# Long attention of a two-branch layer stack: scores ahead of the transposes, and the copies of transposed blocks exchanged between VectorE and ACT

## The reference

```python
xn = _layernorm(x, axis=-1)
x = x + _L0_attn_ref(xn, ...) + _L0_ffn_ref(xn, ...)

# first branch: causal attention, 8 heads in 2 groups of 4, head width 128, keys of latent width 32
q = (x @ wq).reshape(Bq, Tq, N_KV, N_REP, HEAD_DIM)
k = jnp.einsum('bkhl,ld->bkhd', x @ wk_down ..., wk_up)
v = jnp.einsum('bkhl,ld->bkhd', x @ wv_down ..., wv_up)
scores = jnp.einsum('bqhrd,bkhd->bhrqk', q, k) * scale
scores = jnp.where(causal, scores, jnp.finfo(scores.dtype).min)
probs = jax.nn.softmax(scores, axis=-1)
y = jnp.einsum('bhrqk,bkhd->bqhrd', probs, v)
return y.reshape(Bq, Tq, N_HEADS * HEAD_DIM) @ wo

# second branch: six layers, each window attention (16 heads, window 32, rotary) and a gated feed-forward
for i in range(DEPTH):
    x = attn_layer(shift_tokens(x), ...) + x
    x = ffn_layer(shift_tokens(x), ...) + x
```

## Time and profile before

| what | value |
|---|---|
| three runs | 1828.48, 1821.57, 1826.56 us; median 1826.56 |
| the profiled execution, its own time | 1832.16 us |
| its span in the profile | 1830.4 us |
| TensorE (PE) busy | 1633.6 us, 89% |
| VectorE (DVE) busy | 1517.1 us, 83% |
| ACT busy | 1312.9 us, 72% |
| GpSimd (POOL) busy | 1311.1 us, 72% |
| mean granted TensorE clock | 0.975 |

### The profile page before, as it was taken

The page is one execution under the profiler, slowest core; times in us unless marked ns, Lnnn a source line. Parts: engine busy times, 40 slices in busy tenths (PEclk is TensorE's granted clock), DMA queues, the critical chain, the costliest instruction groups (busy, mean ns, idle before and its releaser), DMA issues.

```text
span 1830.4 us, 72588 instructions
## 1 busy us (share of the span) xinstructions
PE 1633.6 (89%) x31192; PEld 1112.7 (61%) x31192; DVE 1517.1 (83%) x1941; ACT 1312.9 (72%) x1868; POOL 1311.1 (72%) x1287
## 2 busy tenths in 40 slices
PE   6777776788999999999999999999999999999995
PEld 5555665455656666666566666656666666666654
DVE  4466566689988999889899989989899998999973
ACT  2465564567788778777877887778777877887773
POOL 3100001888998888898789988889988899888871
PEclk7899999999999999999999999999999999999998
DMA  6011010010000100000100001000010000000000
GB/s 189 11 37 43 17 36 1 4 56 7 8 14 7 56 8 7 11 15 30 33 8 12 15 7 56 7 10 15 8 39 25 7 12 15 7 7 8 7 7 27
DMA packets 47997, 40.61 MB, mean 22 GB/s; under 512 B 33217, under 2 KB 41153, under 8 KB 46017
## 3 DMA queue, kind: packets, MB, share of 16 engines
q1 hardware_dynamic: 47680, 35.98, 7.0%
HBM read 20.22 MB, written 1.05 MB: 12 GB/s over the span
## 4 chain that ended last, share of the span: by engine, by line
PE 44%; issue 24%; DVE 17%; ACT 7%; POOL 6%; SPq 1%; DMA 0%; DVEq 0%; POOLq 0%; ACTq 0%
PE banks L1170 18%; PE banks L1444 10%; PE banks L1393 5%; PE banks L1468 5%; PE banks L1429 4%; DVE arena L1033 3%; DVE lnx L1095 3%; DVE small L1062 2%; DVE small L1068 2%; DVE small L1056 2%; DVE small L1080 1%; ACT L821 1%; ACT arena L755 1%; DVE arena L1028 1%; ACT L824 1%
## 5 line engine op out<-in xcount | busy, mean ns | idle before, releaser
L1444 PE MATMUL banks<-M,xs 128*32 128x512 f32 x3072 | 368.2, 597 | 0.6 <-ACT arena L755 0.3
L1028 DVE TENSOR_TENSOR arena<-banks,tabs 128x1024 f32<-128x1024 f32 x192 | 233.7, 1217 | 39.6 <-ACT arena L715 23.9
L514 POOL TENSOR_TENSOR arena<-arena 128x1024 f32<-128x1024 f32 x96 | 229.7, 2392 | 46.0 <-DVE arena L1033 45.7
L755 ACT ACTIVATE arena<-banks 128x1024 f32<-128x1024 f32 x192 | 196.9, 1025 | 71.1 <-PE banks L1444 69.8
L1033 DVE TENSOR_TENSOR arena<-banks,tabs 128x1024 f32<-128x1024 f32 x192 | 233.0, 1213 | 0.0
L519 POOL TENSOR_TENSOR arena<-arena 128x1024 f32<-128x1024 f32 x96 | 228.1, 2376 | 0.0
L509 POOL TENSOR_TENSOR prob<-prob,small 128x1024 f32<-128x1024 f32 x96 | 183.8, 1914 | 31.5 <-DVE small L1070 31.5
L1095 DVE SCALAR_TENSOR_TENSOR lnx<-lns,small 128x128 f32<-128x128 f32 x96 | 174.4, 1816 | 34.5 <-POOL small L562 33.5
L1170 PE MATMUL banks<-qkH,xsH 128*128 128x512 f32 x384 | 172.8, 450 | 32.3 <-DVE arena L1033 26.5
L1468 PE MATMUL banks<-arena 128*32 128x128 f32 x6144 | 192.3, 278 | 4.2 <-ACT arena L821 4.2
L574 POOL TENSOR_TENSOR arena<-arena,small 128x1024 f32<-128x1024 f32 x96 | 182.8, 1904 | 9.8 <-POOL arena L519 0.5
(11 more groups left out here) (127 smaller groups left out, 3727.0 us busy)
## 6 DMA issues: line engine op xcount, KB each, us to landing
arena<-in_wvo_dram SPq DMA_DIRECT2D x6, 1024.0 KB, 5.3
qkraw<-in_wqk_dram SPq DMA_DIRECT2D x6, 1024.0 KB, 5.3
gq<-w1w SPq DMA_DIRECT2D x64, 64.0 KB, 2.0
lns<-Xt SPq DMA_DIRECT2D x96, 32.0 KB
lns<-Xt SPq DMA_DIRECT2D x96, 31.8 KB
xsH<-w1w SPq DMA_DIRECT2D x32, 64.0 KB, 2.0
xsL<-w1w SPq DMA_DIRECT2D x32, 64.0 KB, 2.0
W<-in_w_dram SPq DMA_DIRECT2D x6, 341.0 KB, 3.2
```

Of the source, the lines that this page charges most:

```text
L514: pool.tensor_tensor(kc, kc, ks, ALU.add).then_inc(s["k_add"], 1)
L755: act.activation(vw[:, (2 * k + g) % RV, :], two(V_BANK), ACT.Copy).then_inc(s[f"v_cp{g}"], 1)
L1028: dve.tensor_tensor(heads(c), heads(two(0)), table(k % NT, kind), ALU.mult).then_inc(s[done], 1)
L1444: ins = pe.matmul(bk(V_BANK + z)[WIN * q:WIN * (q + 1), :], xs[:, b, t0:t0 + WIN], M[:, q, :, :].rearrange("p m n -> p (m n)"), start=True ...
```

## The change

ACT and VectorE exchange the copies: VectorE copies A, ACT copies B and C. On TensorE the long row's scores of t + 2 come first in a step. On VectorE the copy of A is followed by the long row's maximum (t + 2) and then by the short row's (t + 1), and the bookkeeping of every fourth step comes ahead of these.

```diff
 # ACT
-            def first_blocks(t):
+            def last_blocks(t):
+                nb = row_long(t) - 3
+                act.wait_ge(s["gB_mm"], t + 1)
+                act.activation(gptL[t // REP % 2][:, h, 4:4 + nb, :], bk(bank_of(("B", t, 0)))[:, 0:P * nb]..., ACT.Copy).then_inc(s["gB_cp"], 1)
+            def short_blocks(t):
+                nb = row_short(t) + 1
+                act.wait_ge(s["gC_mm"], t + 1)
+                act.activation(gptS[t // REP % 2][:, h, 0:nb, :], bk(bank_of(("C", t, 0)))[:, 0:P * nb]..., ACT.Copy).then_inc(s["gC_cp"], 1)
...
                     if t % REP == 2 and t >= REP:
                         inverses(t // REP - 1)
-                    first_blocks(t)
+                    last_blocks(t)
+                    short_blocks(t)
                     if t + 1 < NSTEP:
                         exp_short(t + 1)
 # VectorE
-            def last_blocks(t):
-            def short_blocks(t):
+            def first_blocks(t):
+                dve.wait_ge(s["gA_mm"], t + 1)
+                dve.tensor_copy(gptL[t // REP % 2][:, h, 0:4, :], bk(bank_of(("A", t, 0)))...).then_inc(s["gA_cp"], 1)
...
                 if t % REP == 0 and t:
                     reciprocals(t // REP - 1)
-                if t + 1 < NSTEP:
-                    peak_short(t + 1)
                 if t % REP == 0 and t >= 2 * REP:
                     add_outputs(t // REP - 2)
                 if t % REP == 2 and t >= REP:
                     scale_outputs(t // REP - 1)
+                first_blocks(t)
                 if t + 2 < NSTEP:
                     peak_long(t + 2)
-                last_blocks(t)
-                short_blocks(t)
+                if t + 1 < NSTEP:
+                    peak_short(t + 1)
 # TensorE
             for t in range(NSTEP):
+                if t + 2 < NSTEP:
+                    score_long(t + 2)
                 turn_first(t)
                 turn_last(t)
                 if t + 1 < NSTEP:
                     score_short(t + 1)
-                if t + 2 < NSTEP:
-                    score_long(t + 2)
                 turn_short(t)
```

More of the change, by code:

```diff
@@ L681, in exp_short @@
                                accum_out=gsum[t // REP % 2][:, REP + h:REP + h + 1]).then_inc(s["gS_exp"], 1)
-            def first_blocks(t):
+            def last_blocks(t):
                 it, p, h = long_at(t)
-                act.wait_ge(s["gA_mm"], t + 1)
-                act.activation(gptL[t // REP % 2][:, h, 0:4, :], bk(bank_of(("A", t, 0))).rearrange("p (k t) -> p k t", k=4), ACT.Copy)\
-                   .then_inc(s["gA_cp"], 1)
+                nb = row_long(t) - 3
+                act.wait_ge(s["gB_mm"], t + 1)
+                act.activation(gptL[t // REP % 2][:, h, 4:4 + nb, :], bk(bank_of(("B", t, 0)))[:, 0:P * nb].rearrange("p (k t) -> p k t", k=nb),
+                               ACT.Copy).then_inc(s["gB_cp"], 1)
+            def short_blocks(t):
+                it, p, h = long_at(t)
+                nb = row_short(t) + 1
+                act.wait_ge(s["gC_mm"], t + 1)
+                act.activation(gptS[t // REP % 2][:, h, 0:nb, :], bk(bank_of(("C", t, 0)))[:, 0:P * nb].rearrange("p (k t) -> p k t", k=nb),
+                               ACT.Copy).then_inc(s["gC_cp"], 1)
             def inverses(q):
@@ L943, in peak_short @@
                 dve.tensor_reduce(gmx[:, 2:3], bk(6)[:, 0:n], AXX, ALU.max, negate=True).then_inc(s["gS_max"], 1)
-            def last_blocks(t):
+            def first_blocks(t):
                 it, p, h = long_at(t)
[L947 to L950, removed]
-            def short_blocks(t):
[L953 to L957, removed]
+                dve.wait_ge(s["gA_mm"], t + 1)
+                dve.tensor_copy(gptL[t // REP % 2][:, h, 0:4, :], bk(bank_of(("A", t, 0))).rearrange("p (k t) -> p k t", k=4))\
+                   .then_inc(s["gA_cp"], 1)
             def reciprocals(q):
```

## The result

The changed kernel took 1771.34 us (median of 4 runs, 1768.50 to 1772.87) against 1827.52 for the kernel before beside it: 0.9694 of its time, 95% interval 0.9665 to 0.9723. The profiled execution took 1768.50 us, with a span of 1766.7.

What follows compares the result with a forecast made beforehand. Bound: TensorE waiting for VectorE's copy of the long row's last blocks. Savings of 34.9 us in 14 stretches plus 3 in the first five steps make 38, giving 1788.5 us after a 5.6 median correction; range 1776 to 1812.

Steps and rivals of the forecast that it cites:

- What bounds the kernel: Long attention: TensorE's transposes wait 40.2 us for VectorE's copy of the last blocks; a microsecond saved there shortens the total.
- The walk's stretches: Long attention, four steps from weighing to weighing without a unit: 12.2 us instead of 14.69, 34.9 saved over 14.
- the ring given for p = 0: Row pair 0: a two-step loop of waits through TensorE, VectorE and ACT takes 4.94 us, steps 2.5 in the mean.
- The first five steps: Start of the long attention, at a mixed clock: 0.6 us saved each, 3 in all (0 to 5).
- a unit costs 2.1: Key and query units in eleven places of the 14 stretches: 2.1 us each, left unchanged.
- The single costs: Instruction lengths: ACT's one-block copy 0.28 us, VectorE's four-block copy 0.68, ACT's work per step some 2.15.
- The bookkeeping: VectorE's add, scale and reciprocals every fourth step, moved ahead: costed at nothing, 0.4 in four steps if not covered.
- (a): ACT's instructions don't overlap in successive copies: 0.2 us a step, 10 to 12 over the stage, 1799; chance 0.15.
- (b): Key or query units wait for ACT's copy: 1.15 us for each of 12, 14 less saved, 1802.5; chance 0.14.
- (c): TensorE becomes the bound in the long attention, its own work 10.5 us per four steps, 1765; chance 0.10.
- (d): TensorE at its lower clock: four steps 16.7 us, +28 over 14 stretches, 1854; chance 0.07.
- (e): The long attention's gain doesn't reach the end: order on TensorE unchanged or later layers eat it, 1826.5; chance 0.04.

Runs made afterwards that it cites:

- e0: The kernel before, unchanged, run again for a second profile; ratio 1.000 (0.9986 to 1.0015).
- e11: The changed kernel, unchanged, run again on another occasion against the kernel before; 1773.58 us, ratio 0.9684.
- e7: The change in steps 0 to 5 alone, the kernel before's arrangement from step 6 on, against the kernel before; 1815.83 us, ratio 0.9920.
- e9: The kernel before, but VectorE copies the long row's remaining blocks ahead of the long maximum, no copy changes engine; 1801.18 us, ratio 0.9843.
- e6: The kernel before with four unused products of 512 columns added on TensorE in each of steps 0 to 4; 1829.27 us, ratio 0.9997.
- e2: The changed kernel's copies and VectorE and ACT order, with TensorE's order of before, against the kernel before; 1791.95 us, ratio 0.9787.
- e3: The changed kernel, but TensorE keeps long scores behind short ones in steps 0 to 5, against the kernel before; 1776.22 us, ratio 0.9700.

## Why the prediction was wrong

The profiled executions of e0 (span 1829.4) and e11 (1774.0) differ by 55.4 us, close to the difference of the medians. Their parts:

| part | forecast | measured | from |
|---|---|---|---|
| steps 0 to 5, to the first weighing | 3 | 11.4 | 65.50 - 54.08; first profiles 15.3; e7 14.4 |
| 14 stretches, without what units cost | 34.9 | 32.5 | 204.8 - 172.3: four each of 14.44 and 14.02, three each of 15.11 and 15.20; now of 12.05, 12.48, 12.82, 11.90 |
| eleven units in them | 0 | 6.2 | 22.2 - 16.0: six in pairs at 4.17 a pair, three at 1.90, two at 2.02; now 3.14, 1.08, 1.68 |
| drops of the clock before | 0 | 4.7 | e0's stretches over those of the earlier trace rows |
| the rest | 0 | 0.6 | 55.4 less the above |

- **What bounds the kernel** held: the copy of B behind the long maximum was the wait (e9 frees it and gains 29 us), and what is saved arrives at the end.
- **The walk's stretches** held: 12.2 in the mean against 12.31. That 11.9 for p = 0 meets 11.90 and 12.5 for p = 3 meets 12.48 is luck in part: the walk took four steps of one p, and a stretch from weighing to weighing has two steps of one p and two of the next (0 and 1, then 2 and 3). And the ring given for p = 0 was the wrong one. Ordinary steps there take 2.20, not 2.5. This did no harm, since behind a weighing the walk itself had steps of 2.18; TensorE is the bound there, busy 11.04 of 11.90 us.
- **The step that failed first**: "The first five steps run at a mixed clock; 0.6 each, 3 in all (0 to 5)". 0.6 is the gain of a stretch divided by four. But in a stretch one step of four had nothing to gain, because the weighing already covered its wait: before, A follows the weighing without idle time (120.61), and after, L comes in between and moves it 0.57 later. The first weighing stands at the end of step 5, so the steps ahead of it gain what an ordinary one does, up to 3.91 - 2.20 = 1.7 at p = 0, and five units lie among them. The clock adds a part: it is 0.82 and 0.69 in the two profiles of before, 0.95 and 0.94 in those of after. The rows had that in them: the prediction read a clock of 0.9 or more in nearly all of the long attention, while the first two of its seven slices, 0 to 91 us, show 7 and 8. How the 11 to 15 us divide is not settled: e6's trace gives the clock 4 to 7 and leaves 7.5 to 9.2 to the arrangement; e6's time gives it at most 3.5.
- **The second**: a unit costs 2.1, "and I leave that as it is". It costs (15.19 - 12.05) / 2 = 1.6 now, 1.1 at step 13 of sixteen (13.56 - 12.48; before 15.92 - 14.02 = 1.9), 1.7 at step 4 (13.58 - 11.90; before 17.22 - 15.20 = 2.0). The stretches of before with the unit of step 13 and with that of step 4:

```profile
87.05:102.97 15.92, 12.03 (x151) 9.79 (x150) 11.03 (x22) 9.95 (x23) 0.00 (x0) 1.00 0.26 63
118.08:135.30 17.22, 11.59 (x152) 9.73 (x151) 10.63 (x21) 9.61 (x23) 0.00 (x0) 1.00 0.01 2
```

Before, the product of the unit behind step 22 waited 1.60 us for B's bank, whose copy stood behind the long maximum; now it follows C at once, and L and A fill the time in which ACT and VectorE finish the unit. The timelines of this unit before, then after:

```profile
141.30 1.12 PE L1170 MATMUL banks<-arena 128*128 128x512 f32 x2 [1.60 <-DVE arena L949]
142.26 0.60 PE L1311 MATMUL banks<-cst,prob 128*128 128x128 f32 x4
143.84 0.55 PE L1311 MATMUL banks<-cst,prob 128*128 128x128 f32 x3 [0.98 <-DVE xnw L904]
```

```profile
113.08 1.02 PE L1170 MATMUL banks<-arena 128*128 128x512 f32 x2
113.54 0.92 PE L1170 MATMUL banks<-xnw,xsL 128*128 128x512 f32 x2
...
114.35 0.62 PE L1311 MATMUL banks<-cst,prob 128*128 128x128 f32 x4
115.76 0.55 PE L1311 MATMUL banks<-cst,prob 128*128 128x128 f32 x3 [0.79 <-DVE xnw L913]
```

- **The third**, small: the stretches of before at a clock below 1.00 were left out of the sum. They cost 4.7 us in e0 and 2.4 in the first profile (16.66 and 18.07 against 15.11 and 17.22). After, every stretch from the first weighing on is at 1.00.
- **The single costs** held: ACT copies one block in 0.27 to 0.29 (L694 and L687; 0.28 taken), VectorE copies four in 0.69. The bookkeeping was rightly put at nothing. ACT is busy 133.03 of 180 us between 70 and 250, 74%, not above 80%: 2.15 us in a step of 2.5 are 86%, but ACT also stands in every weighing, and four times 2.15 in a stretch of 12.2 are 71%.
- **The rivals.** (a) ACT's instructions don't overlap: they do. In ACT's timeline of after each row starts 0.10 or 0.11 before the one ahead of it ends; C's copy, for one, starts 0.48 into B's copy of 0.59:

```profile
203.76 0.37 ACT L680 ACTIVATE arena<-banks,small 128x128 f32<-128x128 f32 x1 [0.60 <-DVE small L952]
204.03 0.19 ACT L680 ACTIVATION_READ_ACCUMULATOR arena<-banks,small 128x1 f32 x1
204.12 1.10 ACT L672 ACTIVATE prob<-banks,small 128x1024 f32<-128x1024 f32 x1
205.12 0.20 ACT L672 ACTIVATION_READ_ACCUMULATOR prob<-banks,small 128x1 f32 x1
205.21 0.59 ACT L687 ACTIVATE arena<-banks 128x512 f32<-128x512 f32 x1
205.69 0.28 ACT L694 ACTIVATE arena<-banks 128x128 f32<-128x128 f32 x1
```

The Trainium skill's bubble between instructions (Advanced Engine Details and Errata, The Read-Write Bubble) isn't seen as a full stop between two of them here: the rows of these six overlap.
- (b) Units wait for ACT: in the unit shown not at all, and from 60 to 245 us their products wait 0.4 for B's copy in two places together. In the head it held more: there units wait 0.35, 0.92 and 0.41 for it. (c) TensorE as the bound, 1765: nearest to the result, and TensorE comes close to it in the stretch of 11.90, with a busy share of 93% (11.04 / 11.90), but its own work there was put at 10.5, and that was not reached. (d) In the long attention the clock fell nowhere; it rose. (e) It did reach the end.

## What to carry to other kernels

In a ring over several in-order engines, a long instruction that looks ahead belongs behind the copy that frees a buffer: exchanging two lines gave half of this gain (e9). A gain per stretch, where a piece of fixed work covers one of the waits, must not be spread to steps that don't have that work; cost the start of a pipeline by itself. And two reorderings may need each other: the scores ahead cost some 6 us alone and saved 17 to 19 with the copies exchanged.

## What the runs showed of the hardware

TensorE's granted clock in the beginning changed with the arrangement of the other engines' work and with work added to TensorE's idle time. With the copies exchanged (after, e11, e2, e3) it was 1.00 from 34 to 54 us, and in after and e11 to the end of the long attention. In the two profiles of the kernel before it was 0.50 to 0.83 in nine of the ten windows of 5 us from 29 to 54, and fell again on the way into p = 0. With twenty more products of 512 columns (e6) it was 1.00 from 34 to 59 us. I had not expected that this would hardly show in the time. In e6's trace the products lie in waits, and the head is 4 to 7 us shorter; but the stretch behind it took 20.28 us at a clock of 0.92, where before took 18.61, and why the median of e6 doesn't follow its profiled execution stays open.
